# Transformer block on one core: query/key/value products as three 16-bit products, copies and a norm moved to GpSimd, new orders

## The reference

```
mod = silu(c) @ wmod                       # sa, ca, ga, sb, cb, gb
h = layernorm(x) * (1 + ca) + sa
q, k, v = split(h @ w_qkv);  q, k = elu(rope(q) * s) + 1, elu(rope(k) * s) + 1
out_t = q_t @ sum_{i<=t} k_i v_i^T / max(q_t . sum_{i<=t} k_i, 1e-6)
x = x + ga * (out @ w_out)
h = layernorm(x) * (1 + cb) + sb
x = x + gb * sum over the two best experts of share * (gelu(h @ w1[e]) @ w2[e])
```

## Time and profile before

| What | Value |
|---|---|
| Time, median of 3 runs | 783.14 us (782.26 to 783.76) |
| Span of the profiled execution | 776.0 us |
| PE, DVE, ACT, POOL busy share of the span | 92%, 81%, 74%, 67% |
| Mean granted TensorE clock | 0.957 |

### The profile page before, as it was taken

How to read it: one execution, slowest core, us unless ns; L and a number is a source line. 1 busy time by engine, 2 the same in 40 slices (tenths; PEclk the granted TensorE clock), 3 DMA queues, 4 the chain that set the end, 5 groups by cost and what they waited for, 6 DMA issues and landing times.

```text
span 776.0 us, 24871 instructions
## 1 busy us (share of the span) xinstructions
PE 714.8 (92%) x8105; PEld 549.7 (71%) x8105; DVE 628.2 (81%) x1494; ACT 571.2 (74%) x1108; POOL 518.5 (67%) x535
## 2 busy tenths in 40 slices
PE   8799999999999999845799999999999999999994
PEld 5467777777777776634677777777777777777772
DVE  4999999999999888778577777777777777777773
ACT  2799899999999998740476767777776767677772
POOL 5777777777777776547466666666666666666642
PEclk9999999999999999855799999999999999999997
DMA  6324344444443412310343343344333333443410
GB/s 226 113 67 133 110 135 120 131 120 139 124 140 116 151 64 67 120 48 8 96 77 69 71 73 74 76 70 79 70 75 69 77 69 76 76 72 76 72 21 1
DMA packets 52854, 69.27 MB, mean 89 GB/s; under 512 B 8864, under 2 KB 44080, under 8 KB 52736
## 3 DMA queue, kind: packets, MB, share of 16 engines
q0 software_dynamic: 18176, 27.06, 18.6%
q1 hardware_dynamic: 34560, 40.61, 16.9%
HBM read 46.50 MB, written 22.05 MB: 88 GB/s over the span
## 4 chain that ended last, share of the span: by engine, by line
PE 51%; DVE 2%; POOL 2%; issue 1%; DMA 1%; ACT 0%; POOLq 0%; DVEq 0%; ACTq 0%
PE hidden L1457 16%; PE bank L1475 15%; PE hidden L1459 8%; PE bank L1477 8%; PE bank L1292 2%; POOL mod_b L960 1%; PE bank L1309 0%; DMA xt<-ffn_rows,gi 0%; DMA out_dram<-x,si 0%; DVE stage L651 0%; PE bank L1300 0%; PE bank L1389 0%; POOL out_dram L1008 0%; DVE feat L652 0%; POOL mod_b L962 0%
## 5 line engine op out<-in xcount | busy, mean ns | idle before, releaser
L1457 PE MATMUL hidden<-qstT,w1hi_k 128*128 128x256 f16 x1136 | 197.9, 274 | 0.7 <-DVE qstT L755 0.7
L1459 PE MATMUL hidden<-qstT,w1lo_k 128*128 128x128 f16 x1136 | 193.6, 220 | 0.0
L1475 PE MATMUL bank<-w,amhi 128*128 x568 | 188.4, 379 | 0.1
L1477 PE MATMUL bank<-w,amlo 128*128 x568 | 154.8, 273 | 0.0
L1008 POOL DMA_INDIRECT out_dram<-x,si x71 | 115.2, 1622 | 38.8 <-issue 25.8
L791 DVE TENSOR_TENSOR amlo<-am,amhi 128x512 f16<-128x512 f32 x142 | 98.3, 693 | 49.2 <-ACT am L1168 49.2
L1457 PEld LDWEIGHTS hidden<-qstT,w1hi_k 128*128 x1136 | 111.7, 98 | 14.0 <-issue 1.1
L1459 PEld LDWEIGHTS hidden<-qstT,w1lo_k 128*128 x1136 | 111.6, 98 | 0.2
L1309 PE MATMUL bank<-wq,hT 128*128 128x512 f32 (+1 forms) x256 | 98.8, 511 | 1.3 <-DVE hT L524 1.2
L1475 PEld LDWEIGHTS bank<-w,amhi 128*128 128x128 f16 x568 | 55.6, 98 | 59.9 <-issue 0.4
L1167 ACT ACTIVATE amhi<-am 128x512 f16<-128x512 f32 x142 | 88.1, 620 | 0.3 <-DVE am L785 0.3
(11 more groups left out here) (219 smaller groups left out, 1783.6 us busy)
## 6 DMA issues: line engine op xcount, KB each, us to landing
stage<-in_L_ffn_w_dram SPq DMA_DIRECT2D x32, 512.0 KB, 4.3
xt<-in_L_attn_x_dram SPq DMA_DIRECT2D x32, 128.0 KB, 4.0
out_dram<-x SPq DMA_DIRECT2D x32, 128.0 KB, 3.7
ffn_rows<-h SPq DMA_DIRECT2D x32, 128.0 KB, 1.8
ffn_rows<-am SPq DMA_DIRECT2D x32, 128.0 KB, 4.2
am<-mod_rows SPq DMA_DIRECT2D x16, 128.0 KB, 4.0
mod_b<-mod_rows SPq DMA_DIRECT2D x8, 256.0 KB, 4.4
w<-in_L_wmod_dram SPq DMA_DIRECT2D x6, 256.0 KB, 4.6
```

The source lines that it names most:

```text
L1457: t.matmul(dst.rearrange("p (q n) -> p q n", q=2), w1s[0][k][g][:, w_], both, start=(k == 0), stop=False)
L1459: last = t.matmul(dst[:, P:2 * P], w1s[1][k][g][:, w_], both[:, 0, :], start=False, stop=(k == KT - 1))
L1475: t.matmul(y[:, :], ghi[:, m.p, c_m], w2s[mt // 2][:, bass.ds(w_, 2 * D)], start=(mt == 0), stop=False)
L1477: last = t.matmul(y[:, D:2 * D], glo[:, m.p, c_m], w2s[mt // 2][:, bass.ds(w_, D)], start=False, stop=(mt == MT - 1))
```

## The change

- `qk` and `v` are made, from chunk 3 on (`PLAIN = 3`), of three 16-bit products for each half of the depth: high by high, high by low, low by high. The weights are split once (`wqh` on ScalarE, `wql` on VectorE, two operations of 128x768 each, in steps 0 to 2). The tile hT gets a high half from ScalarE (`hh`) and a low half from GpSimd (`hl`), so that two more works stand between `hTe` and the products.
- `shq` moves from ScalarE to GpSimd. `slo` becomes one operation of 512 elements instead of two; the stacks' fourth part is zero.
- `xn2` moves from ScalarE to GpSimd, as an operation with two scalars per row.
- The norm tiles (`mv`, `rstd`, `nb`) exist twice, and several waits between `rs`, `nb`, `xn`, `xn2` go or look one step further back. `var` is dropped. hT exists once.
- For chunks 0 to 2 `rope` takes three operations instead of two.
- All order tables are new.

```diff
-ORDER_PE = (("aT", 4), ("ear", 3), ("sc1", 3), ("pj", 4), ("hT", 0), ("h2T", 6), ("Tk", 2), ("pv0", 3), ("v", 0),
-            ("Tq", 2), ("pv1", 3), ("lg", 6), ("state", 2), ("sc0", 2), ("qk", 0))
+ORDER_PE = (("ear", 3), ("sc1", 3), ("hT", 0), ("pj", 4), ("h2T", 6), ("Tk", 2), ("lg", 6), ("v", 0), ("Tq", 2),
+    ("pv0", 3), ("pv1", 3), ("sc0", 2), ("state", 2), ("qk", 0), ("aT", 3))
...
+ORDER_ACT = (("qTs", 3), ("exp", 2), ("sh0", 3), ("whi", 1), ("xn", 0), ("aTe", 4), ("sth", 3), ("sh1", 3),
+    ("hh", 0), ("h2Te", 6), ("kTs", 2), ("lge", 6), ("vhi", 0))
...
             def root(m):
 
                 wait(pool, a_["ve"], m.n + 1)
-                wait(pool, a_["nb"], m.n)
-                wait(pool, a_["xn"], m.n, NC)
-                wait(pool, a_["xn2"], m.n - NORM2)
-                g.tensor_tensor(rstd[:, :], var[:, :], minus_half[:, :], ALU.pow).then_inc(a_["rs"], 1)
+                g.tensor_tensor(rstd[:, m.p, :], rstd[:, m.p, :], minus_half[:, :], ALU.pow).then_inc(a_["rs"], 1)
+
+            def second_normalised(m):
+                wait(pool, a_["h2T"], m.n - 1)
+                wait(pool, s_row[m.p], 16 * m.pairs)
+                wait(pool, a_["nb"], m.n + NORM2 + 1)
+                g.tensor_scalar(h2[:, m.p, :], x1[:, m.p, :], rstd[:, (m.n + NORM2) % 2, 1:2], nb[:, (m.n + NORM2) % 2, 1:2], ALU.mult, ALU.add).then_inc(a_["xn2"], 1)
...
-                g.tensor_tensor(qst[:, :, 1:4:2, :], f[:, 0].broadcast_to([P, NH, 2, HD]), qst[:, :, 0:3:2, :],
-                                ALU.subtract)
-                g.tensor_tensor(kst[:, :, 2:4, :], f[:, 1].broadcast_to([P, NH, 2, HD]), kst[:, :, 0:2, :],
-                                ALU.subtract).then_inc(a_["slo"], 1)
+                g.tensor_tensor(lows, feat[:, :].rearrange("p (q h d) -> p q h d", q=2, h=NH), highs, ALU.subtract)\
+                    .then_inc(a_["slo"], 1)
+
+            def h_low16(m):
+                if m.n < PLAIN:
+                    return
+                wait(pool, a_["hh"], m.n - PLAIN + 1)
+                g.tensor_tensor(h16[:, 1, :], hT[:, :], h16[:, 0, :], ALU.subtract).then_inc(a_["hl"], 1)
...
+            def product16(dst, m, lo):
+
+                for k in range(KT):
+                    hi_, lo_ = (h16[:, c, k * P:(k + 1) * P] for c in range(2))
+                    last = mm3(dst, hi_, lo_, wq16[:, k, 0, lo], wq16[:, k, 1, lo], start=(k == 0), stop=(k == KT - 1))
+                return last
```

More of the change, by code:

```diff
@@ L65 @@
-ORDER_ACT = (("exp", 2), ("sh0", 3), ("shq", 2), ("sth", 3), ("aTe", 4), ("xn", 0), ("sh1", 3), ("whi", 1),
-             ("kTs", 2), ("xn2", 5), ("vhi", 0), ("h2Te", 6), ("qTs", 2), ("lge", 6))
+Q_SCALE = float(HD ** -0.25)
+ORDER_PE = (("ear", 3), ("sc1", 3), ("hT", 0), ("pj", 4), ("h2T", 6), ("Tk", 2), ("lg", 6), ("v", 0), ("Tq", 2),
+    ("pv0", 3), ("pv1", 3), ("sc0", 2), ("state", 2), ("qk", 0), ("aT", 3))
+ORDER_DVE = (("st", 0), ("den", 4), ("mv", 0), ("rec", 4), ("ve", 0), ("at", 4), ("f", 2), ("nb", 0), ("sl0", 3),
+    ("rope", 1), ("hTe", 0), ("stl", 3), ("x1", 4), ("sl1", 3), ("st2", 4), ("mv2", 4), ("wlo", 1), ("vlo", 0))
@@ L67 @@
+ORDER_POOL = (("wb", 5), ("rs", 0), ("shk", 2), ("shq", 2), ("h2", 6), ("slo", 2), ("hl", 0), ("R", 1), ("xn2", 5),
+    ("xm2", 5))
+ORDER_ACT = (("qTs", 3), ("exp", 2), ("sh0", 3), ("whi", 1), ("xn", 0), ("aTe", 4), ("sth", 3), ("sh1", 3),
+    ("hh", 0), ("h2Te", 6), ("kTs", 2), ("lge", 6), ("vhi", 0))
 ORDER_SP = (("ldx", 0), ("modg", 6), ("modb", 7), ("so", 6), ("ro", 6), ("ld", 0), ("modgb", 6), ("gb", 6))
-OPENING_PE = {0: (("hT", 0), ("qk", 0), ("v", 0)), 1: (("hT", 0), ("mod1", 0), ("v", 0), ("qk", 0))}
+OPENING_PE = {0: (("hT", 0), ("qk", 0), ("v", 0)),
+    1: (("hT", 0), ("mod1", 0), ("v", 0), ("qk", 0))}
@@ L69 @@
 OPENING_DVE = {0: (("st", 0), ("mv", 0), ("ve", 0), ("nb", 0), ("hTe", 0)),
-               1: (("st", 0), ("mv", 0), ("ve", 0), ("nb", 0), ("rope", 1), ("vlo", 1), ("hTe", 0), ("wlo", 1), ("vlo", 0))}
-OPENING_ACT = {0: (("xn", 0),), 1: (("xn", 0), ("vhi", 1), ("whi", 1), ("vhi", 0))}
+    1: (("st", 0), ("mv", 0), ("ve", 0), ("wlo", 1), ("nb", 0), ("rope", 1), ("vlo", 1), ("hTe", 0), ("vlo", 0), ("wql", 1)),
+    2: (("st", 0), ("sl0", 3), ("f", 2), ("rec", 3), ("mv", 0), ("sl1", 3), ("ve", 0), ("nb", 0), ("wlo", 1), ("st2", 5), ("hTe", 0), ("rope", 1), ("mv2", 5), ("stl", 3), ("x1", 4), ("vlo", 0), ("den", 3), ("at", 3), ("wql", 1))}
@@ L293, in adaln_block @@
         wmod_raw = [[late(w2s[(k * 3 + j) // 4], (k * 3 + j) % 4 * 512, 512) for j in range(3)] for k in range(KT)]
+        wq_raw = [late(w1s[0][0][k], 0, 3 * D) for k in range(KT)]
         rw_raw = late(w2s[2], 1280, D, E)
@@ L322, in counters @@
             return {k: sem(prefix + k) for k in names.split()}
-        a_ = counters("a_", "st mv ve rs nb xn hT hTe v vhi vlo qk rope R exp f shq shk slo Tq qTs Tk kTs"
+        a_ = counters("a_", "st mv ve rs nb xn hT hTe hh hl v vhi vlo qk rope R exp f shq shk slo Tq qTs Tk kTs"
                             " state sth stl ear sc0 sh0 sl0 sc1 sh1 sl1 pv0 pv1 den rec at aT aTe pj"
@@ L593, in residual @@
                 wait(dve, a_["pj"], m.n + 1)
+                wait(dve, a_["xn2"], m.n - 1)
                 wait(dve, s_out[m.p], 16 * m.pairs)
@@ L613, in _ @@
                 "ve": steadied, "nb": offset, "hTe": h_modulated, "vlo": v_low,
-                "rope": rope, "f": features, "sl0": lambda m: scores_low(m, 0), "sl1": lambda m: scores_low(m, 1),
+                "rope": rope, "wql": qkv_low, "f": features, "sl0": lambda m: scores_low(m, 0), "sl1": lambda m: scores_low(m, 1),
                 "stl": state_low, "den": denominator, "rec": reciprocal, "at": quotient, "x1": residual,
@@ L1045, in earlier_done, with h_high @@
                     wait(act, a_["ear"], (CPB - 1) * prev.b + prev.c)
+            def h_high(m):
+                if m.n < PLAIN:
+                    return
+                wait(act, a_["hTe"], m.n + 1)
+                wait(act, a_["qk"], m.n)
+                wait(act, a_["v"], m.n)
+                copy(h16[:, 0, :], hT[:, :]).then_inc(a_["hh"], 1)
             def v_high(m):
```

160 lines of the change are left out of this document (101 added, 59 removed), and 71 rows, old and new, of tables (CLOSING_ACT, CLOSING_DVE, CLOSING_PE, CLOSING_POOL).

## The result

| | before | after |
| --- | --- | --- |
| Time, median of 5 runs | 783.14 us (782.26 to 783.86) | 788.14 us (786.39 to 791.34) |
| Ratio | | 1.0077, 95% interval 1.0059 to 1.0095 |
| Ratio in a second comparison, in a later session | | 1.0040, interval 1.0016 to 1.0065 |
| Span of the profiled execution | 776.0 us | 789.6 us |

The changed kernel is slower, by 0.4 to 0.8%. The forecast was 792 (772 to 805), slower at 0.60.

A forecast was written before the change was run, and what follows sets the result against it. The prediction had VectorE nearly full and a loop through GpSimd, lengthened by turns at SBUF, setting the step. 783.1 us plus 2.5 (opening), 6.0 (middle) and 0 (closing steps) gave 792; range 772 to 805 for 8 in 10.

The forecast's parts named there:

- the likeliest case: Chunk stage: VectorE and GpSimd take turns, step 9.6 to 9.9 us, time 787 to 798 us; chance 0.42.
- opening: First chunk steps: VectorE's weight split, third `rope` operation and turns with GpSimd cost 2.5 us, between 1 and 4.
- middle: The 26 chunk steps between start and drain: 0.23 us more each, together +6.0 us.
- closing steps: Drain ending the chunk stage: loses TensorE time and ScalarE's `xn2`, gains GpSimd's; 0, plus or minus 3 us.
- Turns between VectorE and GpSimd: Chunk steps: a GpSimd operation beginning inside VectorE's two-input `f` or `wlo` is late by what is left; also the reverse.
- The loop over GpSimd, `nb` waiting for `rs`: Chunk step: chain from `nb` through `hTe`, `hh`, `hl` and GpSimd's queue to the next `nb`; 8.25 us without turns.
- Step 9.77: Chunk step with turns counted: middle of 9.62 and 9.91 us, 0.23 over the 9.54 of before.
- `xn2` at 0.75 alone: GpSimd's scalar operation of 256 in the chunk step: taken at 0.75 us, at least 0.39, at most 1.29.
- `hl` at 0.65: GpSimd's low half of hT in the chunk step, not in the trace: taken at 0.65 us, between 0.58 and 0.73.
- `slo` and `R` as priced: GpSimd operations of the chunk step: single `slo` at 1.12 us, `R` at 1.22 us.
- TensorE's share to 85%: Chunk stage: TensorE's busy share falls from 96% to about 85%, with 1.1 us a step saved.
- VectorE alone bounds, 9.0 to 9.2 us, 772 to 777: Rival for the chunk stage: turns cost little, step 9.0 to 9.2 us, time 772 to 777 us; chance 0.30.

The follow-up runs named there:

- e1: Changed kernel with `wlo` and `whi` put back behind `nb` and `xn` in the opening: 782.22 us, ratio to before 1.0006.
- e5: Changed kernel with the opening's former order and the load of x issued one step earlier: 775.39 us, ratio to before 0.9954.
- e9: Changed kernel with 32-bit products in all chunks, the opening's former order and the load of x one step earlier: 773.45 us, ratio to before 0.9844.
- e6: Changed kernel with 32-bit products in all chunks, without `hh`, `hl` and the weight split: 778.18 us, ratio to before 0.9985.
- e3: Changed kernel with `wlo` right behind `hTe` in VectorE's steady order: 793.67 us, ratio to before 1.0144.
- e12: Kernel before with only `xn2` moved to GpSimd, right ahead of `xm2`: 785.86 us, ratio to before 0.9988.
- e4: Changed kernel with `xn2` back on ScalarE, behind `aTe`, in steady and closing orders: 804.63 us, ratio to before 1.0265.
- e2: Changed kernel with the load of x issued one step earlier, ahead of the store `ro`: 784.03 us, ratio to before 1.0015.
- e7: Changed kernel with one more small power on GpSimd ahead of `xn2`, result unused: 792.74 us, ratio to before 1.0177.

## Why the prediction came out as it did

The direction was right, and 788.14 lies in the likeliest case's own range of 787 to 798, near its lower end: a rise of 8.5 us was forecast, and 5.0 between the medians (3 to 6 by the two ratios) measured. That the sum came so near is luck in part. Its terms were 2.5 (opening), 6.0 (middle) and 0 (closing steps); the profiles have 8.2, 6.0 and -4.3 in the first pair, 8.9, 1.1 and -3.8 in the second.

- **Opening, 2.5 us (1 to 4): wrong, 8.2 to 8.9.** This step failed by what it left out. I priced the new operations (`wql` 0.95 twice: measured 0.95) and did not read the new order of step 1: `wlo` ahead of `nb`, behind a transfer. e1 takes 4.1 us off step 2 and 2.6 to 4.3 off step 5, and its median is level with before. What stays is for the most part the work of the 16-bit weights, the part I had priced: e5 is still 3.7 us later at step 5 than e9, up to 1.2 of which may be the clock (that much the two profiles of before differ in step 2). With the order unmended the weights cost less, 1.9 us between after and e6.
- **Turns between VectorE and GpSimd: right.** `wlo` at 0.88 instead of 0.69, `xn2` at 1.08 or 1.52 instead of 0.55; e3 swaps the victim (`hl` 1.15), e12 shows 1.60. They are paid where VectorE loses them, 0.38 us a step in the first profile of after and 0.18 in the second, and in e12, where GpSimd loses them, they cost nothing. They are not the price of the change by themselves: e9 has `wlo` at 0.81 to 0.90 and the shortest steps of all. Two readings were off: an operation is late by 0.14 to 0.20 us less than what is left of the other (`rs` by 0.38 with 0.52 of `f` left, `xn2` of e12 by 1.06 with 1.26 of `wlo` left), and `nb` is a fourth VectorE operation with two inputs from SBUF.
- **The loop over GpSimd, `nb` waiting for `rs`: wrong.** VectorE never waits there after; GpSimd waits for VectorE, 12.3 us. e4 takes 0.9 us per step from GpSimd, and it goes into that wait. Only when the load of x is out of the way (e2, e5: 2.4 us in 17 steps) or GpSimd has more to do (e7: 4.7) does `nb` wait at all. The loop that I counted is the second limit, close below the first: e7 says that about a third of what is added to it is paid.
- **Step 9.77: hit for the wrong reason.** Measured 9.81 and 9.59. What sets it is VectorE's own queue, longer by the turns, and one wait. In the first profile VectorE is busy 9.31 us of the 9.81 (151.76 us over 16.3 steps) and idle 0.51, of which 0.38 is the wait for x. That wait is a step that I did not have: I took the waits of stores and loads as met, and had not followed SyncE's queue, where a load stands behind a store that waits for GpSimd.
- **Closing steps, 0 plus or minus 3: 4 us better.** Every kernel with the new closing orders has it, e4 and e7 excepted, where GpSimd's or ScalarE's closing work was changed. I have no experiment on its cause.
- **`xn2` at 0.75 alone: 0.55; `hl` at 0.65: 0.67; `slo` and `R` as priced.** The Trainium skill, "GPSIMD Engine Reference", section 4.1 (Engine selection), calls one-input operations on GpSimd roughly line rate, and by that the step was to be 0.2 to 0.3 us shorter. By difference the trace agrees: 0.39 us for 72 elements and 0.55 for 256 is 0.9 ns an element more.
- **TensorE's share to 85%: 86%.** Of the 1.1 us priced per step 0.7 are saved (9.13 busy before, 8.44 after, from the windows; 8.18 in e5), with nothing won by it: e6 gives work back to TensorE and is faster.
- **The likeliest case's range by the sum, "788 to 795":** a step of 9.6 gives 787.2 and not 788, a slip that changes nothing.
- **The rival "VectorE alone bounds, 9.0 to 9.2 us, 772 to 777"** had its step right and its condition missing. The changed kernel has single steps of 9.15; e9 has 9.20 in the mean of all, and 771 us by its ratio. It needs the opening and the load mended and the 16-bit products gone (e5, with them, has 9.35), which a rival about turns could not say.

Still open: why the turns fall more on `wlo` in one execution of the changed kernel than in another, when the orders are the same, and what makes the closing steps shorter. The steps of the changed kernel vary from 9.15 to 11.2 us, those of e9 from 9.03 to 9.27. Waits that come and go and shift the two engines against each other are the likely cause; that is argued and not shown.

## What to carry to other kernels

When work is moved to free an engine, look first at whether the engine that stays loaded ever waited for it. Here TensorE and ScalarE went from 95% to 86%, VectorE stayed at 95%, and the 16-bit form brought two more handovers (`hh`, `hl`) into a chain that had none; taking it out again and mending two places in the orders made a kernel 1.6% faster than before (e9).

Read an order written by hand row by row for what a waiting instruction has behind it, in its first steps and on the DMA queue above all: `wlo` ahead of `nb` in one step cost 2.6 to 4.3 us, as much as all the new operations there, and a load behind a store is as late as the store.

To learn which engine binds, add a small known operation to each and see what part of it comes back in the time. Busy shares of 95% and 83% did not tell that the second counts by about a third. Look also at whether the addition changes what the engines meet: e4 took work from one and lengthened that of the other.
